# Feed-forward of a fused cross-attention and ternary FFN kernel: gate and up multiplied with the weights stationary

## The reference, cut to what matters

```python
def act_quant(x):
    scale = 127.0 / jnp.clip(jnp.max(jnp.abs(x), axis=-1, keepdims=True), EPS)
    return jnp.clip(jnp.round(x * scale), -128.0, 127.0) / scale
def weight_quant(w):
    scale = jnp.clip(jnp.mean(jnp.abs(w)), EPS)
    return jnp.clip(jnp.round(w / scale), -1.0, 1.0) * scale
def h_bitlinear(x, w):
    return jnp.einsum('bsh,oh->bso', act_quant(fwht(x)), weight_quant(w))

x = x + attention(_layernorm(x), ctx_1024)            # ends in out @ Wo, 2048 -> 512
h = _layernorm(x)
gate = h_bitlinear(h, w_gate)                         # 512 -> 2048
up = h_bitlinear(h, w_up)                             # 512 -> 2048
x = x + h_bitlinear(silu(gate) * up, w_down)          # 2048 -> 512
```

## Time and profile before

| | us |
|---|---|
| median of 3 runs (1407.32, 1410.21, 1410.48) | 1410.21 |
| the profiled execution | 1407.37 |
| its span, first to last instruction | 1405.6 |
| mean granted clock of PE | 0.998 |
| PE busy | 1375.1 (98%) |
| DVE busy | 934.7 (66%) |
| ACT busy | 938.9 (67%) |
| POOL busy | 517.0 (37%) |

### The profile page before, as it was taken

One profiled execution on the slowest core, in us unless ns is written; L12 is line 12 of the kernel. 1 busy time (PEld: TensorE's weight loads), 2 busy tenths in 40 slices (PEclk: granted clock), 3 DMA queues, 4 the chain that ended last, 5 costly groups with the idle time before them and its releaser, 6 DMA issues. The chain is left out here.

```text
span 1405.6 us, 25808 instructions
## 1 busy us (share of the span) xinstructions
PE 1375.1 (98%) x8407; PEld 1180.8 (84%) x8407; DVE 934.7 (66%) x2400; ACT 938.9 (67%) x2072; POOL 517.0 (37%) x324
## 2 busy tenths in 40 slices
PE   8999988999999999999999999999989999999998
PEld 8889867999999999999999999998867676776765
DVE  5312046667777777778777787767467677776775
ACT  4556558888888888888888888888634334343332
POOL 0033324432233223332233322235444555645551
PEclk9999999999999999999999999999999999999999
DMA  7767813334433443344443444425443322233211
GB/s 228 224 177 219 234 48 90 100 114 118 131 114 112 134 128 110 118 128 124 119 116 116 124 130 124 118 79 181 129 149 90 76 61 68 62 99 73 61 31 42
DMA packets 173492, 165.05 MB, mean 117 GB/s; under 512 B 81440, under 2 KB 149040, under 8 KB 171568
## 3 DMA queue, kind: packets, MB, share of 16 engines
q1 hardware_dynamic: 166448, 150.82, 38.6%
q10 hardware_dynamic: 6912, 12.59, 2.6%
HBM read 123.44 MB, written 33.01 MB: 111 GB/s over the span
## 5 line engine op out<-in xcount | busy, mean ns | idle before, releaser
L774 POOL TENSOR_TENSOR rk_sp<-ms_sp,neg_half 76x10 f32<-76x10 f32 (+1 forms) x128 | 238.1, 1877 | 555.8 <-DMA ms_sp<-ms 555.8
L996 ACT ACTIVATE pr<-ex,ri 100x361 f32<-100x361 f32 x256 | 153.5, 600 | 64.3 <-DVE ri L1195 64.3
L1205 DVE CUSTOM_DVE_ANT_0 sc<-psS,rk 100x361 f32<-100x361 f32 x256 | 136.3, 533 | 87.5 <-PE psS L849 66.8
L989 ACT ACTIVATE ex<-sc,nb,rq_all 100x361 f32<-100x361 f32 x256 | 175.9, 687 | 5.3 <-DVE nb L1214 5.1
L877 PE MATMUL psZ<-pT_hi,cK_hi 120*128 120x400 f32 (+1 forms) x384 | 133.0, 346 | 0.0
L877 PE MATMUL psZ<-pT_hi,cK_lo 120*128 120x400 f32 (+1 forms) x384 | 131.8, 343 | 0.0
L877 PE MATMUL psZ<-pT_lo,cK_hi 120*128 120x400 f32 (+1 forms) x384 | 131.7, 343 | 0.0
L862 PEld LDWEIGHTS psP<-ident,pr 100*120 100x120 f32 (+1 forms) x768 | 73.2, 138 | 46.0 <-issue 35.3
L849 PE MATMUL psS<-ring_hi,q_hi 128*100 128x362 f32 x256 | 96.7, 378 | 4.1 <-DVE mx L1205 4.0
L1187 DVE TENSOR_TENSOR pT_lo<-psP,pT_hi 122x600 fp32r<-122x600 f32 x128 | 99.0, 774 | 1.8 <-ACT pT_hi L1020 1.6
L1195 DVE RECIPROCAL ri<-rs 100x1 f32<-100x1 f32 x256 | 41.3, 161 | 86.9 <-ACT ex L989 82.8
(11 more groups left out here) (297 smaller groups left out, 3940.2 us busy)
## 6 DMA issues: line engine op xcount, KB each, us to landing
rk<-rk_dram SPq DMA_DIRECT2D x64, 564.1 KB
q_dram<-q_out SPq DMA_DIRECT2D x64, 200.0 KB, 4.8
q_in<-q_dram SPq DMA_DIRECT2D x64, 200.0 KB, 5.1
o_dram<-o SPq DMA_DIRECT2D x64, 200.0 KB, 5.3
stage<-in_w_ff SPq DMA_DIRECT2D x12, 1024.0 KB, 6.3
w_in<-in_w_ff ACTq DMA_DIRECT2D x48, 256.0 KB, 2.4
o_in<-o_dram SPq DMA_DIRECT2D x12, 1024.0 KB, 5.9
cT_in<-in_ctxT SPq DMA_DIRECT2D x15, 361.0 KB, 4.5
```

The lines of the kernel that those rows point to most:

```text
L774: nc.gpsimd.tensor_tensor(rk_sp[:, cols], ms_sp[:, cols], neg_half[0:HG * SKR, :].to_broadcast([HG * SKR, n]), op=ALU.pow).then_inc(g_rk, 1)
L989: nc.scalar.activation(ex[:, h % 2, :], sc[:, h % 2, :], ACT.Exp, bias=nb[:, h % 2:h % 2 + 1], scale=factor(n), accum_out=rs[:, h % 2:h % ...
L996: nc.scalar.activation(pr[:, h, SKP - SK:SKP], ex[:, h % 2, :], ACT.Copy, scale=ri[:, h % 2:h % 2 + 1]).then_inc(a_pr, 1)
L1205: nc.vector.tensor_tensor_reduce(out=sc[:, h % 2, :], in0=psS[0:SQ, 0:SK], in1=rk[:, u % 2, h, :], scale=1.0, scalar=-3.0e38, op0=ALU.mult ...
```

## The change

Gate and up are computed the other way round. The stationary operand is now a 128 x 128 block of the ternary weights and the moving one the 128 tokens, so that hidden values stand on partitions from the start. `hidden_T` and its copies are gone; the turned groups in `half_rot` are split by `high_hT` and `low_hT` where they stand. A token's scale is now a row and not a column: `scales1` writes it over 128 columns (`al_rows`), PE transposes that (`al_T`), ACT copies it (`copy_alT`), and DVE multiplies each gate group by it (`gate`) ahead of ACT's `silu`. The scale of up is taken into `scales2` as `al_up`. POOL's share of the turn within a group is done by group, and one of its two differences across pairs goes to DVE (`rotate_third`). The output projection is split in `out_high` (high part of the heads, two matmuls each, 12 heads ahead of `gate_up`) and `out_low` (16 matmuls in a row behind `gate_up`); `norm_T` now writes `psT[0]`. DVE's `residual` stands ahead of the first `low_hT`, its `statistics` behind the second. POOL moves residuals at the start of a step, behind `ints2`. The last tile uses the same `gate_up` with 64 moving columns, and three more `busy` places are added.

```diff
-        passed = {e: sem(e + "_passed") for e in ("sp", "act", "dve", "pe")}
+        passed = dict.fromkeys(("sp", "act", "dve", "pe"), sem("passed"))
-        AHEAD, FIRST = 6, 10
+        AHEAD, FIRST = 12, 8
...
+            def rotate_within(t, n):
+
+                pool.wait_ge(v_h, t * NB + n + 1)
+                if due(t * NB):
+                    pool.wait_ge(v_hT, t * NB)
+                for k, op in enumerate((ALU.add, ALU.subtract)):
+                    nc.gpsimd.tensor_tensor(half_rot[:, n, k * HB:(k + 1) * HB], hid[:, n, 0:HB], hid[:, n, HB:], op=op
+                                            ).then_inc(g_pair0, 1)
...
-                nc.gpsimd.tensor_tensor(half_rot[:, 2:4, :], hid[:, 0:2, :], hid[:, 2:4, :], op=ALU.subtract).then_inc(g_r2, 1)
+                nc.gpsimd.tensor_tensor(half_rot[:, 3, :], hid[:, 1, :], hid[:, 3, :], op=ALU.subtract).then_inc(g_r2, 1)
...
             def step(i):
+                if i > -2:
+                    if 0 <= i and not last_tile(i):
+                        pool.wait_ge(v_q[1], 2 * i + 2)
+                    move_residuals(i - 1)
...
+            def out_high(t, heads):
+
+                if heads[0] == 0:
+                    pe.wait_ge(a_o, t + (NO - 1))
+                    pe.wait_ge(v_x1, t - 1)
+                for h in heads:
+                    for w in (wo_hi, wo_lo):
+                        nc.tensor.matmul(psA[:], o_hi[:, h, :], w[h // HALF][:, h % HALF, :],
+                                         start=(h == 0 and w is wo_hi), stop=False)
+
+            def out_low(t):
+
+                pe.wait_ge(g_o, t - 1)
+                for h in range(H):
+                    last = nc.tensor.matmul(psA[:], o_lo[:, h, :], wo_hi[h // HALF][:, h % HALF, :],
+                                            start=False, stop=(h == H - 1))
+                last.then_inc(p_out, 1)
...
+            def al_T(t):
+
+                pe.wait_ge(v_scale[0], 6 * t + 6)
+                if due(t):
+                    pe.wait_ge(a_alT, t)
+                nc.tensor.transpose(psT[0][:, 0:TT], al_rows[:], ident[:]).then_inc(p_alT, 1)
...
-                for k in range(2):
-                    for c in range(DC):
-                        last = nc.tensor.matmul(psB[:, 2 * (j % 2) + k, :], q1T[:, c, :],
-                                                wt[:, k, c, j * DIM:(j + 1) * DIM], start=(c == 0), stop=(c == DC - 1))
-                last.then_inc(p_gu, 1)
...
+                width, chunks = (TH, FC // 2) if last_tile(t) else (TT, FC // NB)
+                for k, done in enumerate((p_gate, p_up)):
+                    for i in range(chunks):
+                        col = (j * chunks + i) * P
+                        for c in range(DC):
+                            last = nc.tensor.matmul(psB[:, 2 * (j % 2) + k, i * width:(i + 1) * width], wt[:, k, c, col:col + P],
+                                                    q1T[:, c, 0:width], start=(c == 0), stop=(c == DC - 1))
+                    last.then_inc(done, 1)
...
-            def hidden_T(t, n):
-                if n % 2 == 0:
-                    pe.wait_ge(g_r2 if n else v_r2, t + 1)
...
-                for c in range(DC):
-                    last = nc.tensor.transpose(psT[n % 2][:, c * P:(c + 1) * P], half_rot[:, n, c * P:(c + 1) * P], ident[:])
-                last.then_inc(p_hT, 1)
...
+                    out_high(i + 2, range(AHEAD, H))
+                    out_low(i + 2)
                 if real(i):
                     down(i, 0, front)
                     down(i, 1, front)
                 if real(i + 1):
-                    rotate_hidden(i + 1, 0)
-                    hidden_T(i + 1, 2)
-                    rotate_hidden(i + 1, 1)
-                    hidden_T(i + 1, 3)
+                    for n in range(NB):
+                        rotate_hidden(i + 1, n)
                 if real(i + 2):
                     norm_T(i + 2)
...
-                nc.vector.tensor_tensor(hT_lo[:, n * DC:(n + 1) * DC, :].rearrange("p c t -> p (c t)"), psT[n % 2][:],
-                                        hT_hi[:, n * DC:(n + 1) * DC, :].rearrange("p c t -> p (c t)").bitcast(F32),
-                                        ALU.subtract).then_inc(v_hT, 1)
+                hi, lo = (a[:, n * DC:(n + 1) * DC, :].rearrange("p c t -> p (c t)") for a in (hT_hi, hT_lo))
+                nc.vector.tensor_tensor(lo, half_rot[:, 2 + n if last_tile(t) else n, :], hi.bitcast(F32), ALU.subtract
+                                        ).then_inc(v_hT, 1)
...
+            def gate(t, j):
+
+                dve.wait_ge(p_gate, t * NB + j + 1)
+                dve.wait_ge(a_alT, t + 1)
...
+                nc.vector.tensor_tensor(sil[:, j % 2, :].rearrange("p (i t) -> p i t", t=width),
+                                        psB[:, 2 * (j % 2), :].rearrange("p (i t) -> p i t", t=width),
+                                        alT[:, 0:width].unsqueeze(1).to_broadcast([P, blocks, width]), ALU.mult).then_inc(v_g, 1)
...
+            def silu(t, j):
+                act.wait_ge(v_g, t * NB + j + 1)
+                nc.scalar.activation(sil[:, j % 2, :], sil[:, j % 2, :], ACT.Silu).then_inc(a_sil, 1)
...
+            def rotate_third(t):
+
+                nc.vector.tensor_tensor(half_rot[:, 2, :], hid[:, 0, :], hid[:, 2, :], ALU.subtract).then_inc(v_r2, 1)
```

More of the change, by code:

```diff
@@ L1311, in feed_forward @@
         a_o, v_o, g_o = s("a3_o"), s("v3_o"), s("g3_o")
-        p_out, p_xT, p_rx, p_q1T, p_gu, p_hT, p_rh, p_down = (
-            s(f"p3_{n}") for n in ("out", "xT", "rx", "q1T", "gu", "hT", "rh", "down"))
+        p_out, p_xT, p_rx, p_q1T, p_alT, p_gate, p_up, p_rh, p_down = (
+            s(f"p3_{n}") for n in ("out", "xT", "rx", "q1T", "alT", "gate", "up", "rh", "down"))
         v_x1, v_st, g_rs, v_xn, v_xr = (s(n) for n in ("v3_x1", "v3_st", "g3_rs", "v3_xn", "v3_xr"))
@@ L1479, in step @@
                     inverse_deviation(i + 2)
-                if real(i + 3) and not (isinstance(i, int) and i == -2):
+                if real(i + 3) and i > -2:
                     low_o(i + 3)
[L1482 to L1485, removed]
+                if real(i) and not last_tile(i):
+                    result(i)
             pipeline(pool, step, 3)
@@ L1490, in _, with first_out_proj @@
         def _(pe):
-            def out_proj(t, heads):
-                first = isinstance(t, int) and t == 1
-                if heads[0] == 0:
-                    if not first:
-                        pe.wait_ge(g_o, t - 1)
-                        pe.wait_ge(v_xT, t - 1)
+            def first_out_proj(heads):
                 for h in heads:
-                    if first:
-                        pe.wait_ge(v_o, h // OH + 1)
+                    pe.wait_ge(v_o, h // OH + 1)
                     hi, lo = (w[h // HALF][:, h % HALF, :] for w in (wo_hi, wo_lo))
@@ L1676, in step @@
                 if real(i + 3):
-                    out_proj(i + 3, range(0, 4))
-                if isinstance(i, int) and i == TILES - 3:
+                    out_high(i + 3, range(3, 9))
+                elif i == TILES - 3:
                     busy(psA, 11)
@@ L1681, in step @@
                     q1_T(i + 2)
+                    al_T(i + 2)
                 if real(i + 3):
-                    out_proj(i + 3, range(4, AHEAD))
+                    out_high(i + 3, range(9, AHEAD))
+                elif i == TILES - 3:
+                    busy(psA, 3)
             busy(psT[1], 4)
@@ L1734, in round2, with copy_alT @@
                                      bias=MAGIC, scale=sq[:, 1:2]).then_inc(a_mag[1], 1)
+            def copy_alT(t):
+                act.wait_ge(p_alT, t + 1)
+                if due(t * NB):
+                    act.wait_ge(v_g, t * NB)
+                nc.scalar.activation(alT[:], psT[0][:, 0:TT], ACT.Copy).then_inc(a_alT, 1)
             def copy_q1T(t):
@@ L1768, in step @@
                     if real(i + 1):
-                        silus(i + 1, (j,))
+                        silu(i + 1, j)
                 if real(i + 1):
-                    high_hT(i + 1, 0)
-                    high_hT(i + 1, 1)
+                    for n in range(NB):
+                        high_hT(i + 1, n)
                 if real(i + 3) and not (isinstance(i, int) and i == -2):
@@ L1787, in step @@
                     copy_q1T(i + 2)
+                    copy_alT(i + 2)
                 if real(i + 1):
@@ L2026, in step @@
                 if real(i + 1):
-                    peak(i + 1, 2)
-                    peak(i + 1, 3)
+                    for n in range(1, NB):
+                        peak(i + 1, n)
                 if real(i + 2):
```

239 lines of the change are left out of this document (103 added, 136 removed).

## The result

| | before | after |
|---|---|---|
| median of ten runs each, side by side | 1408.62 (1406.88 to 1410.89) | 1412.16 (1409.12 to 1417.69) |
| ratio | | 1.0032, 95% interval 1.0021 to 1.0043 |
| span of the profiled execution | 1405.6 | 1412.5 |
| distance of the bf16 transposes of two middle tiles | 29.15 | 29.50 |

A forecast was written before the change was run, and what follows sets the result against it. PE set the pace at 29.18 us a tile; DVE's queue would take back half its gain. -1.4 - 0.9 - 10 x 0.6 + 0.1 + 2.7 = -5.5 on 1407.37 gave 1401.9, written as 1403.5; range 1395 to 1418.

The forecast's parts named there:

- PE's sum: PE's work alone in a middle tile: 29.18 - 2.05 + 0.2 + 0.44 = 27.8 us, 1.4 less a tile.
- Gate and up: PE's 128 matmuls a tile, each with a weight load: 128 x 0.057 = 7.30 us, against 6.86.
- That rival: Weight loads of gate and up not hidden: at the skill's 81 ns, 1441 us; chance of anything above 0.064: 0.12.
- The way through DVE, steps 1 to 4: DVE's instructions in a middle tile, from the start of gate and up to the turned norm at 20.6 us.
- The first tile: First tile without f32 transposes, eight `busy` matmuls filling PE's wait: 28.4 us instead of 29.34, -0.9.
- The head: Start of the stage: two heads, six matmuls of 0.23, move behind the first gate and up, -1.4 us.
- step 5: Chain from `norm_T` to the next gate and up: 6.3 to `q1_T`, then 1.9; a tile takes about 28.6 us.
- PE's 20.3: PE's time from gate and up to `norm_T` in a middle tile: 7.3, 5.7, 3.3 and 4.0 us.
- second rival: DVE and POOL block each other at the tile's end, at `ints1`: up to 1.3 us a tile; chance 0.11.
- Last period: The last tile-to-tile period, taken as already 28.4 us before: +0.1 in the sum.
- The last tile: Gate and up 7.3 us instead of 3.64, `rotate_hidden` starting about 2.7 later: +2.7.
- my two bounds: Last tile's gate and up with 64 columns: 7.3 us if fewer columns don't shorten matmuls, or half, 3.6, no loss.

The follow-up runs named there:

- experiment 9: Kernel of experiment 6 with DVE doing the fourth product with up ahead of the split of group 2: 1391.52 us, ratio 0.9894.
- experiment 1: Changed kernel with ACT instead of DVE writing the row of scales (`al_rows`), behind `round1`: 1401.83 us, ratio 0.9963.
- experiment 3: Changed kernel with DVE writing the row of scales behind the rounding `ints1`, no longer ahead of `scales2`: 1400.73 us, ratio 0.9965.
- experiment 6: Changed kernel with ACT writing the row of scales and DVE taking the second peak ahead of `xT_lo`: 1397.16 us, ratio 0.9929.
- experiment 2: Changed kernel with POOL's y addition moved to the next step, behind the last rounding and ahead of the residual moves: 1403.89 us, ratio 0.9983.
- the fourth: Changed kernel with half of the contraction of gate and up left out, 64 matmuls a tile: 1411.08 us in one execution.

## Why the prediction was wrong

**What held.** *PE's sum:* 27.8 forecast; where PE has the same work and doesn't wait ahead of the transposes, in experiment 9, a tile takes 27.90. Gate and up: 7.30 forecast, 7.27 measured. The 81 ns of the Trainium skill (page "TensorE: Matmul & The Clock Gate", section "Back-to-back issue gap") aren't seen: 128 matmuls in a row, each with new fp8 weights, stand 57 ns apart. That rival falls. *The way through DVE, steps 1 to 4,* counted from the start of gate and up (1120.65): `rotate_across` ends at 13.9 (forecast 13.9), the turned norm at 20.4 (20.6), the reduction for the scales starts at 24.2 (24.0 by the sum). The last `ints2` ends at 1.3 (1.4), and from the bf16 transposes to gate and up it is 1.75 (1.9). *The first tile:* its distance fell by 0.6, forecast 0.9. *The head* (from the first `busy` to the first bf16 transposes): forecast -1.4, measured -0.4, but the stretches show another clock:

```profile
1022.80:1031.60 8.80, 8.49 (x33) 6.77 (x33) 4.96 (x13) 4.37 (x7) 2.39 (x3) 0.81 0.87 273
```

for the changed kernel (granted clock 0.81), against experiment 1, which has the same program there, at 1.00:

```profile
1020.30:1028.00 7.70, 7.26 (x33) 5.41 (x33) 4.67 (x12) 4.66 (x8) 2.39 (x3) 1.00 0.84 257
```

Its head took 7.67 us, 1.5 less than the 9.21 of before, whose clock was also 1.00. The term was right. Whether the clock is full at this place changes from execution to execution and is worth 1.1 us: 0.81 and a head of 8.80 to 8.82 in the profiled executions of the changed kernel and experiments 3, 6 and 9, 1.00 and 7.63 to 7.80 in those of the other seven. In the changed kernel's it was 0.50, the lower level, from 1026 to 1028 and 1.00 again from 1030 on; why it fell there no run shows.

**The step that failed** is step 5, the term "2.56, now 2.65 with the row of scales". I added 0.09 for a 128 x 128 instruction, as if it were one more scale of one element, and put its wait for POOL at nothing. By starts it took 1146.19 to 1147.04 = 0.85: 0.19 for itself and 0.66 for POOL, by experiments 2 and 3. `scales2` behind it took 0.88 where it took 0.76 before (1085.69 to 1086.45 in the old trace); it now takes in the scale of up. From the reduction to the transposes it was 3.50, not 2.65. 28.6 + 0.85 = 29.45, against the 29.50 that was measured. It holds in ten periods (the row is not held in the first two tiles and in the last), 8.5 us, of which the held part is 6.6.

That 28.6 fits so well is in part luck. My sum started from PE's 20.3, though the turned norm, which comes last and which `norm_T` waits for, stood at 20.6 in the layout; with it the tile would have been 28.8. `norm_T` started at 20.57, and the two terms behind were 0.03 and 0.15 shorter than forecast, which makes up for most of it.

The second rival had the mechanism but not the place. I asked whether the y addition meets `ints1`, found that it ends 0.3 us earlier, and gave it 0.11. My own layout says otherwise: turned norm at 20.6, `low_o` 4.6, so the y addition lasts from 25.2 to 26.5; the reduction at 24.0 plus 1.3 of small scales puts the row at 25.3, at the start of it. Even `ints1`, which starts 0.47 ahead of the transposes (1147.92 and 1148.39), would by 24.0 + 2.65 stand at 26.2 and meet its end, as it did in experiment 6. I placed the last instruction of a queue against POOL, and that not by my own numbers, and none of those between.

The Trainium skill had the rule: "SBUF — State Buffer", section "Who interferes with whom", names `tensor_scalar` among the operations that can take both port pairs, and I had applied the page only to instructions with two SBUF inputs. The traces agree for the wide row, which is held (0.93 against 0.28); the one-element scale beside the same y addition (0.15 at 1145.99) is not.

**Last period.** Its 29.75 has the same cause at another place. In the last period there is no `low_o` to make, so the y addition comes 4.6 us earlier and meets the normalization. Experiment 1, with `low_o` ahead of the y addition (1334.93) and in the last period (1363.59):

```profile
1334.93 0.54 DVE L1829 TENSOR_SCALAR xn<-x,mv,rstd 128x512 f32<-128x512 f32 x1
...
1363.45 1.38 POOL L1475 TENSOR_TENSOR y<-y,x 128x512 f32<-128x512 f32 x1
1363.59 1.52 DVE L1829 TENSOR_SCALAR xn<-x,mv,rstd 128x512 f32<-128x512 f32 x1
```

Its last distance is 29.56, 0.9 more than the others. In experiment 2, where the y addition isn't there, `xn` takes 0.54 and the last distance is 28.84 like all others. In my sum the last period was "already 28.4 before"; by the transposes it was 29.14 and by gate and up 28.72, a misreading of mine; the sum took only the +0.1 from it.

**The last tile** was forecast at +2.7 and came at +0.5; here the forecast was 2.2 too high. Gate and up of 64 columns, and the second turn's start:

```profile
1386.04 3.69 PE L1582 MATMUL psB<-q1T,wt 128*128 128x64 bf16 x121
1390.06 0.36 PE L1582 MATMUL psB<-q1T,wt 128*128 128x64 bf16 x7 [0.33 <-issue]
...
1396.93 0.39 PE L1604 MATMUL psB<-had,hT_hi 128*128 128x256 f32 x1 [1.34 <-DVE hT_lo L1801]
```

(3.69 - 0.2) / 120 = 0.029 a matmul, against 0.057: half the columns cost half the time. Of my two bounds, 3.6 and 7.3, the lower one was nearly right: gate and up take 4.4 with a wait of 0.33 in them. `rotate_hidden` starts 10.9 us behind gate and up (10.3 before).

**In all:** forecast -5.5; ten periods at +0.36 instead of -0.6, +9.6, of which the excess of step 5 is 8.5; the last period +0.5; the last tile -2.2; head and first tile +1.3. That gives the +3.7 that the stage measured. Where the row isn't in the way, experiments 1 and 3 give ratios of 0.9963 and 0.9965; -5.5 on 1407.4 is 0.9961. That this agrees is again part luck. In experiment 1's trace the head is -1.5 (forecast -1.4), the first distance -0.7 (-0.9), the ten middle ones together -4.9 (-6.0), the last +0.4 (+0.1) and the end +0.5 (+2.7): the last tile's 2.2 too much stand against 1.5 in the others. The sign was turned by a single instruction of 0.28 us of work: with it on the chain but not held (experiment 2) the ratio is 0.9983, with it held 1.0032.

## What to carry to other kernels

When an instruction goes onto a chain, price it by its shape, and lay each instruction of the chain, not only the last, against what POOL does at that moment. Here a wide DVE instruction from SBUF to SBUF beside a POOL addition cost what was left of the addition; order what reads PSUM, or single elements, into that time, or give the row to ACT. And before shortening a stage, ask with an experiment like the fourth, which leaves work out, which engine sets the pace: a gain on an engine that merely waits is none, and a gain ahead of a collision is given back in it.

## What the runs showed of the hardware that I had not expected

- A TENSOR_SCALAR of 128 x 128 with a broadcast input, 0.28 us alone, takes 0.93 or 1.31 beside a POOL TENSOR_TENSOR of 1.29, ending 0.08 or 0.09 us after it; one of 128 x 512 takes 1.52 against 0.54, ending 0.28 after it; one of 128 x 512 that writes bf16 takes 0.62 against 0.42 at its tail. A product with one input in PSUM (0.69 at 1176.29, experiment 9), a reduction of a PSUM bank (0.68 at 1144.89, beside `low_o`) and a scale of one element (0.15 at 1145.99) aren't held.
- ACT writes the same 128 x 128 row in 0.39 us, with or without the y addition beside it.
- TensorE matmuls with new fp8 weights for each: 57 ns apart at 128 columns over 128 of them, 29 ns at 64 columns.
- The granted clock stayed at 1.00 around a wait of 1.38 us with no filler; in the kernel before it was 0.50 from 1045 to 1050, behind the wait of 2.52 us.
